# A fractal mixer's energy moved to VectorE, and its reciprocal made from a ScalarE guess and one Newton step

## The reference, cut to what matters

```
x = (x - xmin) / (xmax - xmin + EPS)                      # EPS = 1e-7
measures = stack([_box_sum(x, k) for k in (2, 4, 8, 16)])
log_m = log(measures + EPS)
alphas = einsum(log_m, lr_c) / sum(lr_c ** 2)             # slope of the logs
a = log_m - log_m.mean(axis=-1);  b = ols_est - ols_est.mean(axis=-1)
sim = (a * b).sum(-1) / (norm(a) * norm(b) + EPS)
x = x * excite
return sim * sigmoid(alpha_norm) + (1.0 - sim) * x
```

## Time and profile before

| what | value |
|---|---|
| median of three runs | 2615.26 us (2614.51 to 2618.99) |
| span of the profiled execution | 2612.6 us |
| box stage, 73.8 to 257.7 us | 183.9 us |
| from there to the first blend operation at 283.9 us | 26.2 us |
| blend stage, 283.9 to 461.7 us | 177.8 us |
| busy over the span: PE, DVE, ACT, POOL | 70%, 66%, 45%, 41% |

### The profile page before, as it was taken

One profiled execution on the slowest core, in us unless ns is written; L12 is line 12 of the kernel. 1 busy time (PEld: TensorE's weight loads), 2 busy tenths in 40 slices (PEclk: granted clock), 3 DMA queues, 4 the chain that ended last, 5 costly groups with the idle time before them and its releaser, 6 DMA issues. The chain is left out here.

```text
span 2612.6 us, 45588 instructions
## 1 busy us (share of the span) xinstructions
PE 1841.8 (70%) x10450; PEld 1310.7 (50%) x10467; DVE 1736.1 (66%) x5126; ACT 1167.3 (45%) x2450; POOL 1064.7 (41%) x993
## 2 busy tenths in 40 slices
PE   1476233399258888299996288919982999929992
PEld 1232133388234344188885144418872544419992
DVE  6998699488757777444443777745657677765664
ACT  2333465277232333155553288804443544416661
POOL 0144133244102434444444216656763045555662
PEclk9777555599679999599998599959996999969996
DMA  2000100121210000122223201113324201113336
GB/s 67 0 1 7 60 23 25 45 62 54 71 66 17 28 26 29 48 67 58 58 58 104 93 12 41 44 47 99 97 72 150 78 28 34 33 55 93 85 89 203
DMA packets 171905, 151.86 MB, mean 58 GB/s; under 512 B 28958, under 2 KB 151590, under 8 KB 171746
## 3 DMA queue, kind: packets, MB, share of 16 engines
q1 hardware_dynamic: 141794, 90.82, 12.5%
q0 software_dynamic: 29952, 59.26, 6.5%
HBM read 83.77 MB, written 68.79 MB: 58 GB/s over the span
## 5 line engine op out<-in xcount | busy, mean ns | idle before, releaser
L1033 POOL DMA_INDIRECT returned<-channel_major x488 | 480.2, 984 | 456.3 <-DVE channel_major L992 323.0
L878 PE MATMUL psum<-channel_major 128*128 128x128 f32 x3360 | 460.6, 277 | 1.1 <-ACT channel_major L925 1.1
L941 ACT ACTIVATE channel_major<-psum,bias_columns 128x128 f32<-128x128 f32 x1104 | 323.1, 367 | 293.3 <-PE psum L878 292.7
L894 PE MATMUL psum<-expert_weights,channel_major 128*128 x2784 | 427.6, 288 | 0.6 <-DVE channel_major L981 0.6
L878 PEld LDWEIGHTS psum<-channel_major 128*128 128x128 f32 x3360 | 420.4, 194 | 1.2 <-issue 1.2
L706 POOL DMA_INDIRECT dispatched<-rows_first_choice,slot x192 | 194.7, 1014 | 547.8 <-DVE rows_second_choice L632 399.2
L894 PEld LDWEIGHTS psum<-expert_weights,channel_major 128*128 128x128 f32 x2784 | 348.9, 191 | 25.1 <-issue 2.0
L706 POOL DMA_INDIRECT dispatched<-rows_second_choice,slot x192 | 196.6, 1024 | 68.6 <-issue 66.8
L992 DVE TENSOR_SCALAR channel_major<-psum,channel_major 128x128 f32<-128x128 f32 x416 | 144.8, 348 | 98.0 <-PE psum L894 93.5
L969 DVE COPY channel_major<-expert_weights 128x512 f32 (+1 forms) x272 | 100.4, 369 | 157.3 <-PE psum L878 147.9
L326 PE MATMUL psum<-identity,rows_first_choice 128*128 128x128 f32 x256 | 42.3, 327 | 195.2 <-DVE rows_first_choice L313 182.6
(11 more groups left out here) (328 smaller groups left out, 3602.0 us busy)
## 6 DMA issues: line engine op xcount, KB each, us to landing
channel_major<-dispatched SPq DMA_DIRECT2D x488, 65.0 KB
expert_weights<-returned SPq DMA_DIRECT2D x12, 1024.0 KB, 10.3
rows_second_choice<-returned SPq DMA_DIRECT2D x8, 1024.0 KB, 10.8
returned<-channel_major POOLq DMA_INDIRECT x488
expert_weights<-in_L_ffn_w SPq DMA_DIRECT2D x3, 2048.0 KB, 9.2
residual<-in_x SPq DMA_DIRECT2D x8, 512.0 KB, 7.2
rows_first_choice<-returned SPq DMA_DIRECT2D x4, 1024.0 KB, 9.0
out<-residual SPq DMA_DIRECT2D x8, 512.0 KB, 6.0
```

Of the source, the lines that this page charges most:

```text
L878: ins = pe.matmul(k.ps[:, PSH + u % 2, j * P:(j + 1) * P], wc[:, u % 2, j * P:(j + 1) * P], xt[:, u % 2, :], start=True, stop=True)
L894: ins = pe.matmul(bank, gs[:, u % HB, j * P:(j + 1) * P], second[:, bass.ds(e, 1), j, :].rearrange("p a c -> p (a c)"), start=(b2 is None ...
L941: ins = act.activation(hs[:, u % HB, cols], k.ps[:, PSH + u % 2, cols], f["act"], bias=bcol[:, bass.ds(e * J + j, 1)])
L1033: pool.indirect_dma_start(out=k.returned[0:N * K, :], out_offset=bass.IndirectOffsetOnAxis(ap=rt[:, u, C:C + 1].bitcast(I32), axis=0), in_ ...
```

## The change

VectorE makes the energy, in its own instruction stream behind the box-8 additions of the next image and after the last slope. ScalarE's `gates` gains a log of (root + 1e-7) and an exponential of its negative, which is a first value of the reciprocal (`guess`). VectorE refines it: t = (root + 1e-7) * guess, then (t - 2) * guess, which is minus the reciprocal; the last subtraction becomes an addition. The multiplication by the slope now stands behind the subtraction, still ahead of `choose`. `mix_root` counts three steps an image. GpSimd keeps only its reduction at the start and the sending.

```
+        guesses = [sqr[2], logs[:, 3, :]]
+            def make_energy(b):
+                c2 = Chain(dve, s["mix_energy"], s["mix_energy"].base + b * 3)
+                dve.wait_ge(*when("mix_squares", 5 * (b + 1)))
+                c2.link(dve.tensor_tensor(sqr[0], sqr[0], sqr[1], ALU.add))
+                c2.link(dve.tensor_tensor(sqr[0], sqr[0], sqr[2], ALU.add))
+                c2.link(dve.tensor_tensor(energy[:, b, :], sqr[0], energy[:, b, :], ALU.mult))
...
                 double(s8, s4, 44, 44, 4)
                 if b:
+                    make_energy(b - 1)
                     dve.wait_ge(*when("mix_contrast", 3 * b))
                 double(s16, s8, 40, 40, 8)
             make_slope(B - 1)
+            make_energy(B - 1)
...
-                dve.wait_ge(*when("mix_root", b + 1))
+                dve.wait_ge(*when("mix_root", 3 * (b + 1)))
-                c2.note(dve.tensor_scalar(logs[:, 0, :], at, 1e-7, None, ALU.add))
+                c2.note(dve.scalar_tensor_tensor(out=logs[:, 0, :], in0=at, scalar=1e-7, in1=guess, op0=ALU.add,
+                                                 op1=ALU.mult))
                 c2.link(dve.tensor_scalar(logs[:, 1, :], xch[:, b, :], lowest[:, b:b + 1], gain[:, b:b + 1],
                                           ALU.subtract, ALU.mult))
                 if b:
                     route.invert(dve, b - 1)
-                c2.link(dve.reciprocal(logs[:, 0, :], logs[:, 0, :]))
-                c2.note(dve.tensor_tensor(logs[:, 0, :], slope[:, b, :], logs[:, 0, :], ALU.mult))
+                c2.note(dve.scalar_tensor_tensor(out=logs[:, 0, :], in0=logs[:, 0, :], scalar=2.0, in1=guess,
+                                                 op0=ALU.subtract, op1=ALU.mult))
                 c2.link(dve.tensor_tensor(logs[:, 2, :], logs[:, 1, :], sig, ALU.subtract))
+                c2.link(dve.tensor_tensor(logs[:, 0, :], slope[:, b, :], logs[:, 0, :], ALU.mult))
                 if b:
                     route.choose(dve, b - 1)
-                c2.link(dve.tensor_tensor(logs[:, 3, :], logs[:, 0, :], logs[:, 2, :], ALU.mult))
+                c2.link(dve.tensor_tensor(logs[:, 2, :], logs[:, 0, :], logs[:, 2, :], ALU.mult))
-                dve.tensor_tensor(at, logs[:, 1, :], logs[:, 3, :], ALU.subtract).then_inc(s["mix_used"].h, 1)
+                dve.tensor_tensor(at, logs[:, 1, :], logs[:, 2, :], ALU.add).then_inc(s["mix_used"].h, 1)
...
-            for b in range(B):
-                c2 = Chain(pool, s["mix_energy"], s["mix_energy"].base + b * 3)
-                pool.wait_ge(*when("mix_squares", 5 * (b + 1)))
-                c2.link(pool.tensor_tensor(sqr[0], sqr[0], sqr[1], ALU.add))
-                c2.link(pool.tensor_tensor(sqr[0], sqr[0], sqr[2], ALU.add))
-                c2.link(pool.tensor_tensor(energy[:, b, :], sqr[0], energy[:, b, :], ALU.mult))
...
                 act.activation(energy[:, b, :], energy[:, b, :], ACT.Sqrt).then_inc(s["mix_root"].h, 1)
+                act.wait_ge(*when("mix_root", 3 * b + 1))
+                act.activation(guesses[b % 2], energy[:, b, :], ACT.Ln, bias=k.eps7).then_inc(s["mix_root"].h, 1)
+                act.wait_ge(*when("mix_root", 3 * b + 2))
+                act.activation(guesses[b % 2], guesses[b % 2], ACT.Exp, scale=-1.0).then_inc(s["mix_root"].h, 1)
```

More of the change, by code:

```diff
@@ L1201, in _ @@
             for b in range(B):
-                at, sig = energy[:, b, :], sqr[b % 2]
+                at, sig, guess = energy[:, b, :], sqr[b % 2], guesses[b % 2]
                 if b:
                     route.add(dve, b - 1)
-                dve.wait_ge(*when("mix_root", b + 1))
+                dve.wait_ge(*when("mix_root", 3 * (b + 1)))
                 c2 = Chain(dve, s["mix_sim"], s["mix_sim"].base + B + b * BLEND)
-                c2.note(dve.tensor_scalar(logs[:, 0, :], at, 1e-7, None, ALU.add))
+                c2.note(dve.scalar_tensor_tensor(out=logs[:, 0, :], in0=at, scalar=1e-7, in1=guess, op0=ALU.add,
+                                                 op1=ALU.mult))
                 c2.link(dve.tensor_scalar(logs[:, 1, :], xch[:, b, :], lowest[:, b:b + 1], gain[:, b:b + 1],
```

## The result

The change makes the kernel slower: 2639.63 us (median of three runs, 2638.22 to 2640.45) against 2615.26. The medians differ by 24.4 us, or 0.93%; the ratio estimated from all the runs is 1.0085, 95% interval 1.0067 to 1.0103. The profiled span grows from 2612.6 to 2636.5 us. The forecast was 2633.0. Medians and ratios here are of executions in the fast state; two single executions far slower than the rest, one of the kernel before and one of experiment 2, are left out of them.

A forecast was written before the change was run, and what follows sets the result against it. It took VectorE to bound the box stage, and in the blend the chain to `choose` through TensorE's gate logits. Terms 2.2 + 15.1 + 0.5 = 17.8 us on 2615.3 gave 2633; range 2620 to 2642.

The forecast's parts named there:

- The bound of the blend stage: Blend: the chain through TensorE's gate logits ends last at `choose`, not the reciprocal; VectorE's idle there becomes about 6 us.
- The blend period: Blend on VectorE: period 25.2 us, 2.52 more per image for six images, +15.1 us.
- the wait in `place`: Blend: VectorE waits 1.98 us per image for the routing's exponential, behind ScalarE's new log and exponential.
- the longer first operation: Blend: the operation ahead of `invert` grows from 0.61 to about 1.15 us, making the chain 0.54 later.
- Two table loads: ScalarE in the blend: log and exponential each take a load of 1283 ns, the routing's exponential none.
- rival B: ScalarE in the blend: log and exponential share one table load, total +8.9 us, 2624; chance 0.28.
- The box stage: Box stage on VectorE: period 24.0 us against 23.98, contention's gain spent on the wait and three operations.
- Rival C: TensorE's clock falls in the new 1.5 us gap before the second contrast, 16.6 us on top, 2650; chance 0.08.
- Rival E: Box stage: no gain from GpSimd's absence, 6 x 5.9 us longer, 2668; chance 0.04 together with anything overlooked.
- the first gate and the first blend: Between stages and first blend: first gate +2.1 us, at 281.2; first `mix_used` at 299.0, +2.2 us.
- the sum of 17.8: First mixer: total lateness of 2.2 + 15.1 + 0.5 us, giving 2633.
- GpSimd's absence: Box stage: without GpSimd beside it, VectorE's own work is 18.06 us an image, 5.9 less than the 23.98 period.

The follow-up runs named there:

- experiment 2: Changed kernel with the energy back on GpSimd as before, keeping the log, exponential and Newton step in the blend: 2631.15 us.
- Experiment 4: Kernel before with its reciprocal replaced by a 1.22 us product, division by the root left out, nothing added on ScalarE: 2611.65 us.
- experiment 5: Changed kernel with ScalarE's log and exponential of the next image moved behind the routing's exponential: 2627.33 us.
- Experiment 8: Changed kernel with an exponential in place of the log, so one table load falls away in each image: 2629.91 us.
- experiment 7: Changed kernel with one unused 128x8 addition on GpSimd behind its reduction at the start: 2635.02 us.
- experiment 1: Changed kernel with the blend put back as before (reciprocal, three-step gates), only the energy moved to VectorE: 2627.87 us.
- experiment 3: Kernel before with four extra VectorE operations, results overwritten, ahead of the box stage as 15.7 us of pure delay: 2632.66 us.
- experiment 12: Kernel before with `invert` of the previous image ahead of the blend's first two operations: 2612.27 us.
- experiment 10: Changed kernel with energy behind box 16, routing's exponential ahead of log and exponential, early tiny GpSimd addition, and `invert` ahead of the blend's first two operations: 2595.69 us.
- experiment 11: As experiment 10, but with the original reciprocal in place of guess and Newton step, without log and exponential: 2599.25 us.
- experiment 6: Changed kernel with make_energy of the previous image behind VectorE's box 16 in place of ahead of it: 2622.84 us.

## Why the prediction was right, and where it was not

The time of 2639.63 lies within the stated range of 2620 to 2642, but above the range of 2628 to 2638 that the forecast gave for its own mechanism. The mechanism in the mixer came out as worked out; the excess is in one term outside the mixer that the sum lacked, and in later layers.

**The bound of the blend stage** was read rightly. The 1.11 us at `choose` meant that work removed ahead of it would turn into idle time; predicted about 6 us, measured 6.41. Experiment 4 shows it with nothing else changed.

**The blend period**, predicted 25.2 us, was 25.1 (six periods: +14.3, predicted +15.1). Of its two parts the wait in `place`, predicted 1.98 and measured 1.89, goes away in experiment 5; what stays there (0.53) fits the 0.54 of the longer first operation.

**Two table loads**, by the eight of eight of the earlier trace rows, was right and rival B false. The Trainium skill's table sets ("ScalarE: Activation LUTs", Table sets: the hidden batching unit) would have let log and exponential share one load; the trace shows one for each, in all eight images. Experiment 8 gives the price of one as 1.28 us a period, with nothing on top: from one load's start to the next ACTIVATE are 345.24 - 343.95 = 1.29 us.

**The box stage** came out as worked out: period 24.0, wait 2.23 (predicted 2.2), gap in TensorE 1.3 to 1.5 from the third image on (predicted 1.5), and border copies at 0.81 to 0.82. Rival C fell with the 1.12 us row; in experiment 7 gaps up to 2.7 us leave the faster level too. Rival E fell with the 0.81 ones.

**Mis-sized: the first gate and the first blend.** I had +2.1 and +2.2 us; the profile shows +1.0 and +1.1 (the last operation of the first blend ends at 297.9, before at 296.8). 0.55 us of it is a box stage that happened to start earlier in this execution (first operation at 73.28, before 73.83). The rest lies in the second image. I took the start of the first energy from the trace of before, as 111.1; here it is 109.41, since the first image's contrasts took 15.46 us in place of 16.66, with a granted clock of 0.90 in place of 0.82 from 88 to 106 us. In four other runs with the energy in this place (those of experiments 1, 5, 7 and 8) these contrasts took 16.07 to 16.97 us, and the gate came at 280.9 to 281.8, near the 281.2 that I had. So the term stands within the scatter of one execution. With it the mixer's +16.2 answers to the sum of 17.8.

**Failed: "GpSimd's absence" was counted as a pure gain.** The prediction followed the three operations to VectorE and never asked what else the first of them did on GpSimd. It carried the engine's switch, at a time when nothing waited for it. That was 4.1 of the 24.4 us, shown by experiments 1 and 7. A row of before held the evidence: the two MODIFY_POOL_CONFIG at L1237.

**Open.** 16.2 and 4.1 make 20.3, the +20.2 at the next norm; the other 3.7 of the profile's 23.9 appear in later layers. From that norm to the end the profiles of all twelve experiments also lose against the one of before, by 0.9 to 7.0 us; among them are experiments 3, 4 and 12 (0.9, 1.3 and 2.6), which change nothing on GpSimd. So part of it may be that the one profiled execution of before ran fast there; no run assigns it to a cause.

So the forecast was near for its own reasons in the larger part. A term too high by about 1.6 us offset some of one of 4.1 left out and of 3.7 unexplained. That the result still fell inside the stated range is partly luck, as the range was not drawn for either of these.

## What to carry to other kernels

Before shortening a long operation, look for idle time behind it on its own engine. If another engine's result ends that idle time, the saving is lost, and whatever was added elsewhere to buy it is paid in full; here replacing the reciprocal pays only once the chain beside it is shorter, by 0.42 us an image in experiments 10 and 11. When work moves into an in-order stream, its place decides: two operations further down turned the energy's move from no gain into one of 16.8 us. When the last ordinary work leaves an engine's early part, look for what its first instruction also did, and leave a tiny one there.

## What the runs showed of the hardware

- GpSimd's first ordinary tensor operation, here behind its early work of another kind, has two MODIFY_POOL_CONFIG in its queue and then several us with nothing shown: 7.3 us ahead of a 128x8 addition alone at the start. Put between the experts' rows and the sum that awaits them, it made the norm behind them 4.0 to 4.8 us late in five kernels.
- Log followed by exponential on ScalarE took two table loads of 1283 ns, in all eight images. Exponential behind exponential, in another part of the code, took none ahead of 348.66 us.
- GpSimd's f32 tensor work beside VectorE's went with slower work on both: a border copy 2.73 us in place of 0.81, GpSimd's own 4.40 against the 2.34 of L284 on the same 128x1024. With VectorE alone and the wait covered (experiment 6) the period of the same work is 21.80 us against 23.98.
- Gaps of 1.0 to 1.5 us in TensorE's work (up to 2.7 in experiment 7) left the faster level standing; idle times of 5.7 us in the same stage did not.
